# A ViT tower kernel: the dynamic convolution's taps gathered compactly, masked and turned on GpSimd, and placed head by head

## The reference

```python
h = patches @ W.T + b                                   # 16 images x 64 patches x 256
v = h @ w1.T + b1
w = softmax((v @ ww.T + bw).reshape(T, B, 16, 31), -1)
vp = pad(v, K - 1 rows of zeros in front)
y = sum over k of w[:, :, :, k:k+1] * vp[k:k + T]       # each head has its own taps
a = layer_norm(h + y @ w2.T + b2) * gamma + beta
h = layernorm(h + a)
g = silu(q(h) @ q(w_gate).T) * (q(h) @ q(w_up).T)
h = layernorm(h + q(g) @ q(w_down).T)
```

## Time and profile before

| | before |
|---|---|
| time of the three runs, us | 127.07, 127.28, 127.78 (median 127.28) |
| span of the profiled execution, first to last instruction, us | 125.7 |
| time of the profiled execution itself | not given; the three runs stand for it |
| TensorE busy | 107.9 us, 86% |
| VectorE busy | 86.1 us, 69% |
| GpSimd busy | 80.8 us, 64% |
| ScalarE busy | 66.1 us, 53% |
| DMA moved | 12.45 MB in 23467 packets, of which 18141 under 512 B |
| GpSimd's L1043 (normalise), eight times | 5.1 us |
| TensorE's L417 (convolution), 256 instructions | 15.8 us |

### The profile page before, as it was taken

One profiled execution on the slowest core, in us unless ns is written; L12 is line 12 of the kernel. 1 busy time (PEld: TensorE's weight loads), 2 busy tenths in 40 slices (PEclk: granted clock), 3 DMA queues, 4 the chain that ended last, 5 costly groups with the idle time before them and its releaser, 6 DMA issues.

```text
span 125.7 us, 2379 instructions
## 1 busy us (share of the span) xinstructions
PE 107.9 (86%) x718; PEld 67.8 (54%) x718; DVE 86.1 (69%) x202; ACT 66.1 (53%) x109; POOL 80.8 (64%) x153
## 2 busy tenths in 40 slices
PE   6997999999999999999999999999998653884400
PEld 2673465866856486467555576668573322453200
DVE  5014593644965768799998999888696676898410
ACT  0042128639527444594633988766783836575200
POOL 6994000059700865867974868798888888888870
PEclk9999999999999999999999999999999999689975
DMA  3899999962321122232313112212300100011112
GB/s 104 260 357 340 399 420 422 400 255 21 63 24 17 42 25 23 53 51 42 32 42 30 14 42 25 22 42 27 64 0 0 42 0 0 4 46 42 44 43 82
DMA packets 23467, 12.45 MB, mean 99 GB/s; under 512 B 18141, under 2 KB 21981, under 8 KB 23070
## 3 DMA queue, kind: packets, MB, share of 16 engines
q1 hardware_dynamic: 21936, 10.46, 29.4%
q10 hardware_dynamic: 1518, 1.84, 4.8%
HBM read 9.95 MB, written 2.34 MB: 98 GB/s over the span
## 4 chain that ended last, share of the span: by engine, by line
PE 63%; POOL 19%; issue 5%; DMA 4%; ACTq 2%; DVE 2%; POOLq 1%
PE bank L339 12%; PE bank L417 11%; PE bank L400 11%; PE bank L383 6%; PE bank L444 5%; POOL q L1080 5%; DMA bias_cols<-in_cols 4%; PE bank L472 4%; PE bank L488 3%; POOL rstd L999 3%; POOL f L1087 3%; PE bank L357 3%; ACTq L676 2%; POOL res L1055 2%; POOL veps L998 2%
## 5 line engine op out<-in xcount | busy, mean ns | idle before, releaser
L339 PE MATMUL bank<-xT,tokW 128*128 128x256 f32 x72 | 16.7, 381 | 0.0
L417 PE MATMUL bank<-conv_w,vpad 128*32 128x128 f32 x256 | 15.8, 398 | 0.0
L1043 POOL TENSOR_TENSOR taps<-probs,inv_total 128x256 f32<-128x256 f32 x8 | 5.1, 634 | 15.7 <-DVE inv_total L741 15.4
L339 PEld LDWEIGHTS bank<-xT,tokW 128*128 128x128 f32 x72 | 13.5, 190 | 2.6 <-issue 0.9
L400 PE MATMUL bank<-wl,h1T 128*128 128x496 f32 x32 | 14.6, 578 | 0.0
L641 ACT ACTIVATE gu<-bank,sc 128x512 f32<-128x512 f32 x16 | 11.0, 686 | 5.3 <-PE bank L472 5.1
L527 PE MATMUL bank<-w_q,q2T 128*128 128x256 f16 x64 | 8.5, 273 | 3.9 <-ACT q2T L655 3.5
L812 DVE TENSOR_TENSOR gu<-gu,bank 128x512 f32<-128x512 f32 x16 | 10.8, 681 | 1.3 <-ACT gu L641 0.6
L998 POOL TENSOR_SCALAR veps<-mv 128x1 f32<-128x1 f32 x16 | 3.6, 225 | 11.9 <-DVE mv L751 10.9
L417 PEld LDWEIGHTS bank<-conv_w,vpad 128*32 128x32 f32 x256 | 8.3, 122 | 5.2 <-issue 1.4
L1080 POOL TENSOR_SCALAR q<-gu,sc 128x512 f16<-128x512 f32 x14 | 10.0, 716 | 1.4 <-DVE sc L829 0.2
(11 more groups left out here) (119 smaller groups left out, 237.2 us busy)
## 6 DMA issues: line engine op xcount, KB each, us to landing
xT<-in_xT SPq DMA_DIRECT2D x3, 768.0 KB, 16.9
w_raw<-in_wg SPq DMA_DIRECT2D x1, 1024.0 KB, 13.2
w_raw<-in_wu SPq DMA_DIRECT2D x1, 1024.0 KB, 15.2
w_raw<-in_wd SPq DMA_DIRECT2D x1, 1024.0 KB, 16.9
shear<-taps SPq DMA_DIRECT2D x8, 128.0 KB, 1.8
conv_w<-shear SPq DMA_DIRECT2D x64, 16.0 KB, 2.0
out_dram<-res SPq DMA_DIRECT2D x8, 128.0 KB
tokW<-in_tokW SPq DMA_DIRECT2D x6, 128.0 KB, 5.0
```

The costliest lines, as they stand in the source:

```text
L339: last = nc.tensor.matmul(ps_embed(pair, m), tokW[:, k, m * P:(m + 1) * P], xT[:, pair, k, :], start=(k == 0), stop=(k == KC_PATCH - 1))
L417: last = nc.tensor.matmul(ps_yT[j * SLOT:(j + 1) * SLOT, k, :], vpad[:, s, h, :], conv_w[:, s, :, h], start=(par == 0), stop=(par == 1))
```

## The change

The taps' way from GpSimd to `conv_w` and the order of the indices of `conv_w` are changed:

- `conv_w` is [partition, slot, head, column] instead of [partition, slot, column, head]: the 128 columns of one head's matrix lie side by side, 4 B apart. The matmul of `conv(t)` reads `conv_w[:, s, h, :]`.
- `put_taps(t)` stores `taps` in another DRAM layout: a row for each image, in which the position of a patch moves by one tap from image to image.
- `gather(t)`, new on SyncE: one DMA reads for each of 128 partitions 16 pieces of 64 B into a compact tile `near[partition, 16, head]`.
- `near_mask(t)`, new on GpSimd: multiplies `near` by a mask `inside` (1 where the tap lies in the triangle, 0 elsewhere) and writes it with the head outside, `near_h[partition, head, 16]`.
- `place(t)`, in place of `spread(t)`: eight DMAs, one for each patch, from `near_h` in SBUF to the block diagonal of `conv_w`.
- The mask is made at the start: 16 small memsets and an iota on GpSimd, three small operations on VectorE.
- SyncE's list and GpSimd's list are written out anew; TensorE's, ScalarE's and the rest of VectorE's stay.

```diff
 BLOCK = P // IMAGES
 QUADS, SLOT = 4, 32
-ROW = 2 * IMAGES - 1
+SHEAR_ROW = P * HEADS + IMAGES * HEADS
 PAIRS, UNITS = TILES // 2, TILES
 BIASES = LOGITS + 2 * D
...
         total = sb("total", [P, 2, HEADS])
         inv_total = sb("inv_total", [P, 2, HEADS])
         taps = sb("taps", [P, 2, IMAGES, HEADS])
-        conv_w = sb("conv_w", [P, SLOTS, P, HEADS])
+        conv_w = sb("conv_w", [P, SLOTS, HEADS, P])
+        near = sb("near", [P, 2, IMAGES, HEADS])
+        near_h = sb("near_h", [P, 2, HEADS, IMAGES])
+        inside = sb("inside", [P, IMAGES])
+        lag = sb("lag", [P, IMAGES])
+        place_i = sb("place_i", [P, 1], i32)
+        place_f = sb("place_f", [P, 1])
         yT = sb("yT", [P, 2, KC, P])
         stats = sb("stats", [P, 3, 2, 6])
         mv = sb("mv", [P, 3, 2, 2])
...
                 sp.dma_start(out_d[:, t * BLOCK:(t + 1) * BLOCK, :].rearrange("i b d -> b i d"),
                              res[:, t % 2, :]).then_inc(out_done[t % 2], 16)
-            row = ROW * HEADS
+            row = IMAGES * HEADS
             def put_taps(t):
-                base = shear_d.offset + (t % 2) * P * row
+                base = shear_d.offset + (t % 2) * IMAGES * SHEAR_ROW
                 sp.wait_ge(taps_ok, t + 1)
-                if t >= 2:
-                    sp.wait_ge(conv_in[(t - 2) % SLOTS], 16 * BLOCK * ((t - 2) // SLOTS + 1))
-                sp.dma_start(bass.AP(shear_d.tensor, base, [[row, P], [1, IMAGES * HEADS]]),
-                             taps[:, t % 2].rearrange("p k h -> p (k h)")).then_inc(taps_out[t % 2], 16)
-
-            def spread(t):
-
-                s = t % SLOTS
-                base = shear_d.offset + (t % 2) * P * row
-                sp.wait_ge(taps_out[t % 2], 16 * (t // 2 + 1))
                 if t == 0:
                     sp.wait_ge(tails_in, 16)
+                if t >= 2:
+                    sp.wait_ge(near_in[t % 2], 16 * (t // 2))
+                sp.dma_start(bass.AP(shear_d.tensor, base + HEADS, [[row, BLOCK], [SHEAR_ROW + HEADS, IMAGES], [1, row]]),
+                             taps[:, t % 2].rearrange("p k h -> p (k h)")).then_inc(taps_out[t % 2], 16)
+
+            def gather(t):
+
+                base = shear_d.offset + (t % 2) * IMAGES * SHEAR_ROW
+                sp.wait_ge(taps_out[t % 2], 16 * (t // 2 + 1))
+                if t >= 2:
+                    sp.wait_ge(near_ok, t - 1)
+                sp.dma_start(near[:, t % 2], bass.AP(shear_d.tensor, base + row,
+                                                     [[HEADS, P], [SHEAR_ROW, IMAGES], [1, HEADS]])
+                             ).then_inc(near_in[t % 2], 16)
+
+            def place(t):
+
+                s = t % SLOTS
+                sp.wait_ge(near_ok, t + 1)
                 if t >= SLOTS:
                     sp.wait_ge(yT_ps, t - SLOTS + 1)
                 for b in range(BLOCK):
                     at = b * IMAGES
-                    window = bass.AP(shear_d.tensor, base + at * row + (IMAGES - 1) * HEADS,
-                                     [[HEADS, IMAGES], [row - HEADS, IMAGES], [1, HEADS]])
-                    sp.dma_start(conv_w[at:at + IMAGES, s, at:at + IMAGES, :], window).then_inc(conv_in[s], 16)
+                    sp.dma_start(conv_w[at:at + IMAGES, s, :, at:at + IMAGES],
+                                 near_h[at:at + IMAGES, t % 2]).then_inc(conv_in[s], 16)
             sp.wait_ge(pool_zeros_ok, 1)
-            sp.dma_start(bass.AP(shear_d.tensor, shear_d.offset + IMAGES * HEADS,
-                                 [[row, P], [P * row, 2], [1, (IMAGES - 1) * HEADS]]),
-                         conv_w[:, SLOTS - 1].rearrange("p m h -> p (m h)")[:, 0:2 * (IMAGES - 1) * HEADS]
+            sp.dma_start(bass.AP(shear_d.tensor, shear_d.offset + P * HEADS,
+                                 [[SHEAR_ROW, IMAGES], [IMAGES * SHEAR_ROW, 2], [1, row]]),
+                         conv_w[0:IMAGES, SLOTS - 1].rearrange("p h m -> p (h m)")[:, 0:2 * row]
                          .rearrange("p (s z) -> p s z", s=2)).then_inc(tails_in, 16)
             sp.dma_start(xT[:, 3], xT_d[3]).then_inc(x_in[3], 16)
-            put_taps(0); spread(0); put_taps(1); spread(1); put_taps(2); spread(2); put_taps(3); spread(3)
-            put_taps(4); spread(4); put_taps(5); spread(5); put_taps(6); spread(6); put_taps(7); spread(7)
+            put_taps(0); gather(0); put_taps(1); place(0); gather(1); place(1); put_taps(2); put_taps(3); gather(2)
+            gather(3); place(2); place(3); put_taps(4); gather(4); place(4); put_taps(5); gather(5); place(5)
+            put_taps(6); gather(6); place(6); put_taps(7); gather(7); place(7)
             store(0); store(1); store(2); store(3); store(4); store(5); store(6); store(7)
             for slot in range(2):
                 sp.wait_ge(out_done[slot], 16 * TILES // 2)
...
                         for j in range(QUADS):
                             h = (k * QUADS + j) * 2 + par
                             last = nc.tensor.matmul(ps_yT[j * SLOT:(j + 1) * SLOT, k, :], vpad[:, s, h, :],
-                                                    conv_w[:, s, :, h], start=(par == 0), stop=(par == 1))
+                                                    conv_w[:, s, h, :], start=(par == 0), stop=(par == 1))
                 last.then_inc(yT_ps, 1)
                 put["conv"] += 1
...
                 bias_rows(0, LOGITS)
             nc.vector.memset(vpad[:], 0.0).then_inc(zeros_ok, 1)
+            dve.wait_ge(place_ok, 1)
+            after(mark(nc.vector.tensor_scalar(place_i[:], place_i[:], IMAGES - 1, None, ALU.bitwise_and)))
+            after(mark(nc.vector.tensor_copy(place_f[:], place_i[:])))
+            nc.vector.tensor_scalar(inside[:], lag[:], place_f[:, 0:1], -0.5, ALU.subtract,
+                                    ALU.is_gt).then_inc(inside_ok, 1)
             dve.wait_ge(cols_in, 16)
             nc.vector.tensor_copy(b1_rep[:], b1.unsqueeze(2).broadcast_to([P, KC, P])).then_inc(b1_rep_ok, 1)
             dve.wait_ge(const_ok, 1)
...
                                         inv_total[:, s].unsqueeze(2).broadcast_to([P, HEADS, IMAGES]),
                                         ALU.mult).then_inc(taps_ok, 1)
+            def near_mask(t):
+
+                s = t % 2
+                if t == 0:
+                    pool.wait_ge(inside_ok, 1)
+                pool.wait_ge(near_in[s], 16 * (t // 2 + 1))
+                if t >= 2:
+                    pool.wait_ge(conv_in[(t - 2) % SLOTS], 16 * BLOCK * ((t - 2) // SLOTS + 1))
+                nc.gpsimd.tensor_tensor(near_h[:, s].rearrange("p h m -> p m h"), near[:, s],
+                                        inside[:].unsqueeze(2).broadcast_to([P, IMAGES, HEADS]),
+                                        ALU.mult).then_inc(near_ok, 1)
+
             def result(t):
                 pool.wait_ge(rstd_out, t + 1)
...
             nc.gpsimd.memset(ones_bf[:], 1.0).then_inc(ones_ok, 1)
             nc.gpsimd.memset(ones[:], 1.0)
+            for d in range(IMAGES):
+                nc.gpsimd.memset(lag[:, d:d + 1], float(d))
+            link(nc.gpsimd.iota(place_i[:], pattern=[[0, 1]], base=0, channel_multiplier=1))
+            nc.gpsimd.memset(halves[:, 1:2], 0.5).then_inc(place_ok, 1)
             nc.gpsimd.memset(minus_half[:], -0.5)
             nc.gpsimd.memset(halves[:, 0:1], -0.5)
-            nc.gpsimd.memset(halves[:, 1:2], 0.5)
             nc.gpsimd.memset(minus_magic[:], -MAGIC)
             nc.gpsimd.memset(magic[:], MAGIC)
             nc.gpsimd.memset(minus_step[:], -STEP)
...
                                          pattern=[[-1, P]], channel_multiplier=1))
             nc.gpsimd.tensor_copy(ident16[:], ident[:]).then_inc(const_ok, 1)
             nc.gpsimd.memset(conv_w[:], 0.0).then_inc(pool_zeros_ok, 1)
-            normalise(0); weight_round(0); weight_clip(0); normalise(1); weight_finish(0, wq_gate_ok)
-            inv_std_attn(0); normalise(2); add_beta(0); normalise(3); inv_std_mid(0); add_beta(1)
-            inv_std_attn(1); inv_std_mid(1); normalise(4); add_beta(2); weight_round(2); inner_limit(0)
-            inv_std_attn(2); inner_limit(1); scale_h3(0); inv_std_mid(2); weight_clip(2); add_beta(3)
+            normalise(0); weight_round(0); weight_clip(0); normalise(1); near_mask(0)
+            weight_finish(0, wq_gate_ok); near_mask(1); inv_std_attn(0); normalise(2); add_beta(0); normalise(3); inv_std_mid(0); add_beta(1)
+            inv_std_attn(1); near_mask(2); inv_std_mid(1); near_mask(3); normalise(4); add_beta(2); weight_round(2); inner_limit(0)
+            inv_std_attn(2); inner_limit(1); near_mask(4); scale_h3(0); inv_std_mid(2); weight_clip(2); add_beta(3)
             quant_inner(0, 0); normalise(5); scale_h3(1); inner_limit(2); quant_inner(0, 1); inv_std_attn(3)
-            weight_finish(2, wq_down_ok); scale_h3(2); inv_std_mid(3); normalise(6); quant_inner(1, 0)
```

(7 more changed lines are left out.)

6 lines of the change are left out of this document (5 added, 1 removed).

## The result

The changed kernel takes 150.91 us (median of 4 runs, 150.72 to 151.11) against 127.17 us (126.81 to 127.78) of the kernel before on the same chip: 1.1865 times as long, 95% interval 1.1801 to 1.1928. It is slower, as forecast, but by 23.7 us where 11.2 were forecast: 150.9 lies above the range of 133.5 to 142.5.

The account below looks back on a forecast made before the run. TensorE's length was taken to bound the kernel up to 91 us, GpSimd's queue after it. Span 125.7 plus GpSimd's 11.2 us delay from late taps gave 136.9, plus 1.6 around the span 138.5 us; range 133.5 to 142.5.

Parts of the forecast that it names:

- The eight placing DMAs have the packets of the old spreads: Placing taps into conv_w: like the old spreads, 5.3 us from first issue to last landing, SyncE held for 3.75 us.
- the placing DMAs being a little faster (they now read SBUF): Placing into conv_w: possible gain used to stretch the range down to 133.5 us, below the 135.2 us case.
- the full half: TensorE's convolutions: packed columns halve each from 1.88 to 1.0 us, a gain of 0.87 us on each of eight.
- no gain from packing: Rival for the convolutions: four tiles side by side set the rate, each stays at 1.88 us; total 139.4 us, chance 0.08.
- Store, 2.2 us: SyncE's store of the taps to DRAM: landing rises from 1.75 to 2.2 us; lower bound 1.75.
- Gather, 3.5 us between 2.8 and 4.1: New SyncE DMA of 2048 packets of 64 B: 3.5 us to landing, the middle of its bounds.
- Mask, 0.74: Masking on GpSimd, 256 elements: 0.74 us, eight times; bounds 0.63 and 0.8 us.
- The start at nothing: Making the mask on GpSimd and DVE in the first 10 us, during load waits: costs nothing, uncovered under 1 us.
- GpSimd's end keeps its delay: GpSimd's queue after tile 7's mask: gaps of some 0.1 us, so 11.2 us late is kept to the end.
- The clock falls: Rival: TensorE's idle waits lower its granted clock, adding 2 to 4 us, 141 to 143; chance 0.08 shared with upper bounds.
- Faster: Rival: placed taps arrive before TensorE asks; about 126.0 us remains; chance 0.04.

Follow-up runs that it names:

- e13: Kernel before, the eight spreads of each tile given another source and destination form (device memory or chip, one piece or apart) from tile to tile: 126.99 us, one run.
- e11: Changed kernel with four placing DMAs of 32 partitions in place of eight of 16, mask kept twice, whole function computed: 137.75 us, ratio 1.089.
- e1: Kernel before, the convolution reading 128 consecutive numbers instead of every sixteenth, taps' way unchanged, values not the reference's: 124.76 us, ratio 0.983.
- e8: Kernel before, each tile's convolution reading its columns at another stride, 4 to 48 bytes apart: 125.02 us, one run.
- e5: Kernel before, DRAM side of the taps' store arranged as 8 groups of 16 rows, same bytes and spreads: 127.52 us, ratio 1.002.
- e10: Kernel before plus eight mask-sized multiplications on unused tiles at the masks' places in GpSimd's list: 128.53 us, ratio 1.012.
- e7: Changed kernel with the mask set to ones by one memset, everything that makes it left out, masks still applied: 151.51 us, ratio 1.182.
- e4: Changed kernel with one placing DMA of 128 partitions in place of eight, same bytes but not on the diagonal: 131.85 us, ratio 1.038.
- e12: Changed kernel, placing DMAs reading a weight in device memory instead of the masked taps on the chip, destination kept: 151.02 us, ratio 1.190.
- e3: Changed kernel with rows of near_h 17 numbers long, so both sides of each placing DMA are 64 B pieces: 151.51 us, ratio 1.190.
- e6: Changed kernel with near_h rows 17 numbers apart and each placing DMA writing one 1 KB piece per partition: 151.00 us, ratio 1.189.
- e2: Changed kernel, the convolution reading every sixteenth number again (64 B apart), taps still coming the new way: 152.75 us, ratio 1.193.

## Why the prediction was wrong

The direction, the mechanism (late taps delay TensorE, then GpSimd's list) and the places of the waits were right; the size was not. The step that failed, the mis-sized term, is **"The eight placing DMAs have the packets of the old spreads (256 of 64 B): 5.3 us from first issue to last landing, SyncE held for 3.75"**. Measured: 6.6 us (97.73 to the convolution at 104.34) and 5.2 us, since each issue takes 0.65 us with a source on the chip (e13). Equal packets do not mean equal issues. No run has the new way with the old spacing, so what this term is worth in the whole is an estimate: SyncE is held 2.6 us per tile in e11 (137.75 us) and 5.2 in the changed kernel (150.91), and on a straight line between them 3.75 us give 143.6. That makes 7 of the 12.4 us by which the forecast missed; the late start, the clock and GpSimd's load are left for the rest. The range even reached down for "the placing DMAs being a little faster (they now read SBUF)"; reading the chip made them slower.

How 1.5 us per tile become 7 by the fourth tile, along the prediction's own steps:

| step | predicted | measured | where the difference comes from |
|---|---|---|---|
| store 0 issued | 26.0 | 27.96 | +1.95, the load of the biases |
| placing 0, first issue | 33.4 | 34.57 | store, gather and mask 0.8 shorter together |
| gather 1 issued | 37.2 | 39.91 | SyncE held 1.5 longer |
| convolution 1 starts | 46.7 | 50.30 | gather 0.4 shorter, landing 1.3 longer |
| placing 2, first issue | 52.2 (57.5 less 5.3) | 55.79 | unchanged, +3.6 |
| store 4 issued | 59.7 | 66.83 | two placings hold 10.94, not 7.5 |
| mask 4 | 65.4 | 72.51 | +7.1 |

Of the 7.1 us the placing has 1.5 + 1.3 + 3.4 = 6.2, the start 1.95, and store, gather and mask give 1.2 back. From there the difference grows further, with 1.5 us of SyncE for each placing and with the clock: GpSimd late by 15.1 against 7.5 at `inv_std_attn(3)`, 21.6 against 11.2 at the last of the earlier trace rows, and 23.5 at the end.

The other steps, one by one.

- **Packing, 1.88 to 1.0 us, "the full half"**: right at full clock, 1.08, and for the reason given (e1, e8). The mean of a matmul was to be near 280 ns and is 332, by the convolutions at the lower clock. The rival "no gain from packing" fell.
- **Store, 2.2 us**: 2.8. It was read from the output's half-busy engines; the longer issue (0.6 us, not 0.33) was left out (e5).
- **Gather, 3.5 us between 2.8 and 4.1**: 2.8, the lower bound. Counting 2048 packets at the 10.4 ns of the earlier trace rows came out. The 2.3 us by the formula of the Trainium skill (DMA: Bandwidth & Descriptors, "Anatomy of one DMA — SWDGE (gpsimd) path") were too short by 0.5; the Trainium skill fits that formula to DMAs that GpSimd issues, and this one is SyncE's. Store and gather together were forecast at 5.7 and measured at 5.6, so their errors cancel.
- **Mask, 0.74**: right (72.51 to 73.24). That GpSimd's load as such costs something was not said, and e10 gives it 1.5 us.
- **The start at nothing**: the first store is 1.95 us late. It is the load of the biases that landed late, and with e7 the making of the mask is not shown to have a part in it.
- **GpSimd's end keeps its delay**: nearly. It grew from 21.6 to 23.5, where 11.2 was carried through unchanged. The prediction took convolution 7 to be off GpSimd's path; the chain that ended last in the changed kernel goes through tile 7's placing (109.26), convolution 7 (116.83) and the projection to GpSimd.
- **The clock falls**: it did, at convolution 2 already and at 6, in part at 3 and 7. It was to add 2 to 4 us. TensorE is busy for 110.3 us in the changed kernel and for 101.7 in e1, with the same 718 matmuls and packed columns in both, so 8.6 us of its work are longer; how much of that reaches the end no run measured. It goes with the long waits: in e4, where they are 5.3 us in all, the convolutions average 294 ns against 332.
- **Faster**: the rival needed store, gather, mask and placing inside 7.1 us; e4, with 9.2, is still 4% slower than before.

## What to carry to other kernels

Cost a DMA by who issues it, how often, and where its source lies, not by its bytes alone: here a series of eight DMAs from on-chip memory cost 0.65 us each of one queue, with 16 KB or 64 in them, and that times eight stood in front of the next tile's store. A layout that halves one engine's time per tile (0.9 us) is no gain when the way to it is 5.9 us longer (2.8 + 2.8 + 0.7 + 6.6 against 1.75 + 5.3). Of two variants with the same work, first look at the air ahead of each use: some 1.5 us more per placing cost nothing in three tiles of e13 and, by the estimate above, some 7 us here.

## What was not expected of the hardware

- Eight DMAs of 16 KB issued from SyncE: 0.46 to 0.49 us apart from device memory, 0.63 to 0.66 from on-chip memory, and 0.65 from device memory too where the source is one run and the destination is pieces apart (e13, e12). Cutting either side into 64-byte pieces changed nothing (e3, e6), nor did four times the bytes in each (e11).
- At full clock TensorE reads a moving operand of f32 at nearly full rate with 8 bytes from column to column (1.15 us against 1.08), in 1.58 with 12 and in 2.0 from 16 to 48 (e8). At 1.2 GHz the packed columns take 1.93 and those 64 bytes apart 2.07 (e2).
- A gather of 2048 pieces of 64 B lands 2.8 us after its issue, no later than a store of the same 128 KB in 128 pieces of 1 KB whose destination begins with a dimension of 8.
- After 4.6 and 6.7 us without a matmul TensorE's clock was at 1.2 GHz for the next convolution, and behind the longer one for the eight matmuls and the projection that followed as well (1.92 and 1.91 us).
